# Last stage with sixteen packed expert tiles in place of eighteen, and the first stage's end in another order

## The chip, the cores and the metric

The kernel runs on one core of one Trainium2 chip. The metric is the device time of the whole program in microseconds (us). TensorE is called PE, VectorE DVE, ScalarE ACT, GpSimd POOL and SyncE SP, as in the profile.

## The reference: what is computed

Input is 32 sequences of 750 x 64. Patches of 16 steps with stride 8 become L = 92 tokens of width D = 128 (2944 tokens in all), through a linear layer and a layernorm. Then come two layers, each an attention part and a feed-forward part on a normalized stream, with a residual. Layer 0: a state-space scan with 16 states and a six-expert layer that sends each token to one expert. Layer 1: a local attention with 7 neighbours and 16 heads, and a dense mixture of six experts that this change is about:

```python
probs = softmax(x.mean(axis=1) @ router_w.T)            # one decision per sequence
vals, idx = top_k(probs, 2); vals = vals / vals.sum()
expert_weights = einsum('bk,bke->be', vals, pw[idx])     # 6 weights per sequence
h = gelu(einsum('bsd,edf->ebsf', x, W1) + b1)            # 6 experts, 341 hidden columns each
out_e = einsum('ebsf,efd->ebsd', h, W2) + b2
out = einsum('be,ebsd->bsd', expert_weights, out_e)
```

## The kernel before

Work is tiled in NCH = 8 chunks of 4 sequences (CB = 4, CT = 368 tokens), features on the partitions. Every engine runs its own list in program order, and semaphores tie the lists together. Five stages follow each other, each ended by `stage_end`.

**First stage** (to about 90 us). For each chunk: the patch matmuls (`embed`), a transposition to token-major, a normalization that ACT writes (`embed_norm`), DVE's gamma and beta (`scale_row`, `shift_row`), statistics of the result (`stream_stats`, `stream_moments`), a power on POOL, DVE's `stream_norm`, ACT's `norm_second`, transpositions back, ACT's copies (`norm_copies`), the delta matmul, and on ACT `softplus`. The three chunks in flight are c, c-1, c-2 and c-3 in one turn of the loop. `first_minus` and `first_plus` are ACT exponentials for state 0 of the scan, of which the stage after needs the result; the half for chunks 0 to 3 stands in turn c = 8, behind the softplus of chunk 5. The last things on ACT's list are `softplus(7)`, `first_minus(7, 8)`, and then a table load and the first tanh of the scan stage (L777, L847).

**Last stage** (from about 554 us). In turn c the stage works on attention of chunk c, on the projection, router and first experts of chunk f = c-1, and on the other experts and output of chunks c-2 and c-3.

- PE, in this order: `qkv_of(c)` (L1972), expert tiles of c-2, `project(c-1)` (L1981), more tiles with `result_tm(c-3)` between them (L1953), `scores(c)` (L1991, L1995), tiles, `scores_tm` (L2002), tiles, `shares_fm` (L2008), two tiles, the transpositions of chunk c-1 (L263), then seven steps of `spread_out(c, o)` (L2023, L2024) with tiles between them, `router_spread` (L2033) and tiles.
- An expert of 341 hidden columns is three tiles of 128, 128 and 85. A tile of layer 1 is three matmuls (L1934 to L1936, a number split in high and low parts), a tile of layer 2 is one (L1942, which the trace shows as two records). `FFN` is the list of the 36 tiles of a chunk in the order in which PE takes them, and `ffn(f, lo, hi)` issues a part of it. ACT applies the gelu to each tile of layer 1 (L1008).
- DVE: `weigh_expert` multiplies an expert's output by its weight (L1478), POOL adds it up (L708, `add_expert`). For the attention: the score products (L1509), the softmax (L1524 to L1536, with ACT's exponential and two table loads between them), and for each of seven offsets three products, one of 344 columns and two of 12 for the ends of the sequences (L1599), which POOL adds up (L738). `spread_out(o)` waits until offset o-2 has been read.
- Between the offsets stands the router on tiles of 4 x 11 (L1463, L1457, L1467, L1560 to L1580), and with it `stream_sums`, `weigh_expert` 4 and 5.

Of the kernel before, what the change touches and what calls it, by code (L numbers as in the profile page):

```python
# [7 lines left out]
def audio_tower(nc, t, out):  # L8
# [27 lines left out]
    FT = 3  # L36
    FR = FF - 2 * D
# [24 lines left out]
    with ctx:  # L62
# [203 lines left out]
        def norm_copies(act, nm, u, c, banks, scale=None, bias=None, dst=xfm, hi=None):  # L266
            for w in range(nm.n):
# [48 lines left out]
        split_hi = sb("split_hi", [128, NE * FF], f32r)  # L316
        split_lo = sb("split_lo", [128, NE * FF], f32r)
        w_hi, w_lo = (x[:, 0:8 * D].rearrange("p (s u k d) -> p s u k d", s=2, u=2, k=2) for x in (split_hi, split_lo))
        v1_hi, v1_lo = (x[:, :].rearrange("p (e f) -> p e f", e=NE) for x in (split_hi, split_lo))
# [100 lines left out]
        W_COLS = 3 * D + D + K * 2 * HEADS + K * D + OH + CT + NE * FF + 3 * NE * D + NE + NE + NE * NPART + NE * CB + D  # L420
# [8 lines left out]
        v1 = take(NE, FF)  # L429
        v2 = take(NE, 2, D)  # L430
        v2b = take(NE, D, parts=FR)
        b1b = take(NE, parts=FR)
# [27 lines left out]

        fh = take(3, FT, CT)
        facc = take(CT)
# [13 lines left out]
        ewb = take(NE, CB)  # L476
        bb = take(CB)
# [8 lines left out]
        facc_add = sem("facc_add")  # L486
        f_mm, f_free = sem("f_mm"), sem("f_free")
# [7 lines left out]
               + [(1, e, j) for e in (3, 4) for j in range(FT)] + [(2, e, j) for e in (2, 3) for j in range(FT)]  # L495
               + [(1, 5, 0), (1, 5, 1)] + [(2, 4, j) for j in range(FT)] + [(1, 5, 2)]
               + [(2, 5, j) for j in range(FT)])
# [7 lines left out]
        def _(sp):  # L505
# [42 lines left out]
            for dst, name in ((v1, "v1"), (v2, "v2"), (v2b, "v2b"), (b1b, "b1b"), (b2T, "b2T"), (pwT, "pwT"),  # L548
                              (diag, "diag"), (ones4, "ones4")):
                sp.dma_start(dst, t[name]).then_inc(wF_ready, 16)  # L550
# [54 lines left out]
        def _(pool):  # L605
# [92 lines left out]
            def add_expert(f, e):  # L698
                if not 0 <= f < NCH:
                    return  # L700
                if e == 0 and f:
                    pool.wait_ge(fT_ready, f)
                pool.wait_ge(fo_free, f * NE + e + 3)
                if e:
                    pool.wait_ge(facc_add, f * NE + e + 2)
                a3, t3 = (x.rearrange("p (j l) -> p j l", j=CB) for x in (facc, ftmp[:, e % 2]))
                other = bb.rearrange("p (j o) -> p j o", o=1).to_broadcast([D, CB, L]) if e == 0 else a3
                pool.tensor_tensor(a3, t3, other, ALU.add).then_inc(facc_add, 1)  # L708
# [36 lines left out]
            for c in range(NCH + 2):  # L745
                add_expert(c - 3, 5)
# [4 lines left out]
                add_expert(c - 2, 0)  # L751
# [5 lines left out]
                add_expert(c - 2, 4)  # L757
                if c < NCH:
# [7 lines left out]
        def _(act):  # L766
# [244 lines left out]

# [23 lines left out]
            for c in range(NCH + 2):  # L1035
# [6 lines left out]
                gelus(c - 2, 18, 21)  # L1042
# [3 lines left out]
                gelus(c - 2, 27, 33)  # L1046
# [1150 lines left out]
```

## Time and profile before

| | us |
|---|---|
| median of three runs (857.26 to 857.68) | 857.44 |
| the profiled execution's own time | 858.12 |
| its span | 856.3 |
| PE busy over the span | 632.5 |
| DVE busy | 630.3 |
| ACT busy | 519.7 |
| POOL busy | 268.0 |

Busy time is the union of an engine's instructions; the granted clock of PE is 1.00 at 2.4 GHz and 0.50 at 1.2 GHz. In a row of the order of time the first number is the start and the second the length in us.

### The profile page before, as it was taken

To read this page: it belongs to the slowest core of one execution; us is meant where nothing else is said; L and a number is where in the kernel's file an instruction comes from. 1 tells how busy PE (TensorE), PEld (TensorE's weight loads), DVE (VectorE), ACT (ScalarE), POOL (GpSimd) and SP (SyncE) were. 2 spreads that over 40 slices of the span, in tenths; PEclk is the share of its full clock that TensorE was granted. 3 is DMA by queue.
4 is the path that set the end of the run, shared out by engine and by line. 5 is a ranking of instruction groups with operands and counts; after the bars stand their busy time and mean duration, and the time that the engine had idled before them with its cause. 6 is when DMAs were issued, how large, how long until landed. Compare 5 with 4: busy or idle time off the path is not lost.

```text
span 856.3 us, 10989 instructions
## 1 busy us (share of the span) xinstructions
PE 632.5 (74%) x3150; PEld 484.1 (57%) x3151; DVE 630.3 (74%) x1351; ACT 519.7 (61%) x813; POOL 268.0 (31%) x297
## 2 busy tenths in 40 slices
PE   6994752652816537297773799877999999999987
PEld 4552752652816537274652789534766766766655
DVE  1785597999999999997874112268788888887752
ACT  1587999999899898952322234244465565464432
POOL 0464100000000000101486244314545556464432
PEclk9995776876869677699685799978899999999999
DMA  5380043444455543434112466200000000000000
GB/s 174 113 302 22 0 83 70 77 77 83 83 92 109 93 83 70 75 66 161 68 30 83 115 170 170 60 27 1 1 1 9 1 10 10 1 10 10 0 10 19
DMA packets 26273, 56.51 MB, mean 66 GB/s; under 512 B 4006, under 2 KB 15375, under 8 KB 26004
## 3 DMA queue, kind: packets, MB, share of 16 engines
q0 software_dynamic: 5728, 24.56, 15.2%
q1 hardware_dynamic: 19924, 30.88, 12.0%
q10 hardware_dynamic: 576, 0.52, 0.2%
q8 instruction: 21, 0.34, 0.2%
q14 instruction: 24, 0.20, 0.1%
HBM read 29.89 MB, written 10.17 MB: 47 GB/s over the span
## 4 chain that ended last, share of the span: by engine, by line
PE 42%; DVE 24%; issue 15%; ACT 9%; DMA 3%; POOL 3%; POOLq 1%; SPq 1%; DVEq 0%; ACTq 0%
PE psum L1942 10%; DVE s_R L1197 5%; DVE s_R L1184 4%; PE psum L1672 4%; DVE s_R L1208 3%; PE psum L1934 2%; PE psum L1865 2%; PE psum L1972 2%; DVE s_R L1599 2%; PE psum L1873 2%; DVE s_R L1189 2%; DMA s_R<-x_sorted 2%; PE psum L263 2%; PE psum L1936 2%; PE psum L1995 2%
## 5 line engine op out<-in xcount | busy, mean ns | idle before, releaser
L1736 PE MATMUL psum<-s_xn_lo,s_split_hi 128*128 128x368 f32 x256 | 95.6, 374 | 135.3 <-ACT s_R L882 132.8
L1736 PEld LDWEIGHTS psum<-s_xn_lo,s_split_hi 128*128 128x128 f32 x256 | 55.3, 216 | 140.0 <-ACT s_R L882 135.5
L1942 PE MATMUL psum<-s_R 128*128 128x368 f32 (+1 forms) x288 | 101.2, 477 | 4.1 <-ACT s_R L1008 4.1
L1203 DVE TENSOR_TENSOR_SCAN s_R<-s_R 128x2944 f32<-128x2944 f32 x16 | 100.7, 6291 | 0.8
L650 POOL DMA_DIRECT2D s_xnfm<-s_R x14 | 17.1, 1219 | 255.9 <-DVE s_R L1208 255.9
L1737 PE MATMUL psum<-s_xn_hi,s_split_lo 128*128 128x368 f32 x256 | 92.6, 362 | 0.0
L1738 PE MATMUL psum<-s_xn_hi,s_split_hi 128*128 128x368 f32 x256 | 92.2, 360 | 0.0
L1008 ACT ACTIVATE s_R<-psum,s_cols 128x368 f32<-128x368 f32 x96 | 50.6, 566 | 53.1 <-PE psum L1936 52.8
L708 POOL TENSOR_TENSOR s_R<-s_R 128x368 f32<-128x368 f32 x47 | 44.9, 956 | 74.7 <-DVE s_R L1478 55.0
L1942 PEld LDWEIGHTS psum<-s_R 128*128 128x128 f32 (+1 forms) x288 | 51.2, 189 | 28.6 <-issue 8.2
L738 POOL TENSOR_TENSOR s_R<-s_R 128x368 f32<-128x368 f32 x48 | 46.7, 973 | 57.1 <-DVE s_R L1599 55.7
L889 ACT ACTIVATE s_R<-psum,s_cols 128x736 f32<-128x736 f32 x64 | 55.8, 875 | 13.6 <-PE psum L1738 9.3
L1934 PE MATMUL psum<-s_xn_lo,s_split_hi 128*128 128x368 f32 x144 | 59.2, 411 | 4.8 <-DVE s_xn_lo L1540 2.3
L1184 DVE SCALAR_TENSOR_TENSOR s_R<-s_R 128x2944 f32<-128x2944 f32 x16 | 51.4, 3213 | 9.7 <-ACT s_R L847 5.9
L882 ACT ACTIVATE s_R<-psum,s_cols 128x736 f32<-128x736 f32 x64 | 55.5, 875 | 2.1 <-PE psum L1738 1.4
L1197 DVE SCALAR_TENSOR_TENSOR s_R<-s_R,s_mean 128x2944 f32<-128x2944 f32 x16 | 52.5, 3282 | 5.2 <-ACT s_part L873 3.9
L1737 PEld LDWEIGHTS psum<-s_xn_hi,s_split_lo 128*128 128x128 f32 x256 | 55.2, 216 | 0.0
L1738 PEld LDWEIGHTS psum<-s_xn_hi,s_split_hi 128*128 128x128 f32 x256 | 54.8, 214 | 0.0
L1672 PE MATMUL psum<-s_R 128*128 128x368 f32 x128 | 45.7, 503 | 7.1 <-ACTq L772 7.1
L1208 DVE SCALAR_TENSOR_TENSOR s_R<-s_R,s_A_c 128x2944 f32<-128x2944 f32 x15 | 49.2, 3282 | 0.6
L1936 PE MATMUL psum<-s_xn_hi,s_split_hi 128*128 128x368 f32 x144 | 48.4, 336 | 0.0
L1935 PE MATMUL psum<-s_xn_hi,s_split_lo 128*128 128x368 f32 x144 | 48.4, 336 | 0.0
(245 smaller groups left out, 1562.5 us busy)
## 6 DMA issues: line engine op xcount, KB each, us to landing
s_xnfm<-s_R POOLq DMA_DIRECT2D x14, 1472.0 KB, 10.5
s_R<-in_w SPq DMA_DIRECT2D x28, 256.0 KB, 2.9
s_R<-in_xg SPq DMA_DIRECT2D x7, 744.0 KB, 4.2
x_sorted<-in_x_init SPq DMA_DIRECT2D x1, 5082.0 KB
s_wBC<-in_wBC SPq DMA_DIRECT2D x8, 256.0 KB, 2.7
s_R<-x_sorted SPq DMA_DIRECT2D x28, 66.0 KB
s_R<-in_w SPq DMA_DIRECT2D x1, 1536.0 KB, 6.3
s_R<-y_rows SPq DMA_DIRECT2D x8, 184.0 KB
```

Source lines behind the costliest of these rows:

```text
L889: act.activation(group(bufC, u, h), psum[:, h * HB:(h + 1) * HB, 0:CT], ACT.Silu, bias=cols[:, bass.ds(n + at["C_b"], 1)], scale=1.0).then ...
L1184: dve.scalar_tensor_tensor(th[:, u], ea, 1.0, th[:, u], ALU.add, ALU.mult).then_inc(ea_free, 1)
L1197: dve.scalar_tensor_tensor(bufB[:, u], bufB[:, u], mean[:, u:u + 1], th[:, u], ALU.subtract, ALU.mult).then_inc(th_free, 1)
L1203: dve.tensor_tensor_scan(bufB[:, u], ra[:, u], bufB[:, u], 0.0, ALU.mult, ALU.add).then_inc(ra_free, 1)
L1208: dve.scalar_tensor_tensor(bufC[:, u], bufB[:, u], A_c[:, bass.ds(n, 1)], bufC[:, u], ALU.mult, ALU.mult).then_inc(prod_ready, 1)
L1672: ins = pe.matmul(bank(u).rearrange("p (b l) -> p b l", b=CB), w_emb[:, j, h, :], x4[:, j, :, h:h + L], start=(n == 0), stop=(n == 7))
L1736: pe.matmul(bank(c), w_hi[:, s, u, k, :], xn_lo[:, a:b], start=True, stop=False)
L1737: pe.matmul(bank(c), w_lo[:, s, u, k, :], xn_hi[:, a:b], start=False, stop=False)
L1738: ins = pe.matmul(bank(c), w_hi[:, s, u, k, :], xn_hi[:, a:b], start=False, stop=True)
L1934: pe.matmul(o, w_hi_, fm(xn_lo, f % 2), start=True, stop=False)
L1936: pe.matmul(o, w_hi_, fm(xn_hi, f % 2), start=False, stop=True).then_inc(f_mm, 1)
L1942: ins = pe.matmul(bank((2, 4)[e % 2]), w, fh[0:kk, e % 3, j], start=(j == 0), stop=(j == FT - 1))
```

## The change

Of each expert, the first 256 hidden columns stay as two tiles. The six remainders of 85 columns (510 columns) are packed side by side into NR = 4 tiles of 128, so that a chunk has 12 + 4 = 16 tiles in each layer. A packed tile holds columns of several experts, so its gelu is multiplied by the expert weights before layer 2 (`weigh_rest`, one DVE instruction over 4 x 368 columns, with a mask that gives each hidden column its expert's weights), and the four packed tiles of layer 2 add up to a seventh unit whose output ACT copies out (`rest_out`). The output bias b2 moves into `weigh_expert`. PE's tiles and the others' lists are dealt out anew. PE gets three matmuls without a reader in front of `shares_fm` from turn 2 on, and some in the last turns of the first stage. The two products for the ends of an offset become one. In the first stage ACT's `first_minus(0, NP)` moves in front of `embed_norm(7)`, `first_plus(0, NP)` in front of `norm_second(6)`, and DVE's work on chunk 7 in front of `stream_norm(6)`.

```diff
+        FFN: ... [(1, 3, 0), (1, 3, 1)] + [(1, NE, r) for r in range(NR)]
+               + [(1, 4, 0), (1, 4, 1)] + [(2, e, j) for e in (2, 3) for j in range(FT)]
+               + [(1, 5, 0), (1, 5, 1)] + [(2, e, j) for e in (4, 5) for j in range(FT)]
+               + [(2, NE, r) for r in range(NR)])
 # ACT, first stage
                 if c == NCH - 1:
+                    act.wait_ge(A_ready, 1)
+                    first_minus(0, NP)
                     embed_norm(c)
+                if c == NCH:
+                    first_plus(0, NP)
                 if c >= 2:
                     norm_second(act, nA, c % 2, c - 2)
...
-                if c == NCH:
-                    act.wait_ge(A_ready, 1)
-                    first_minus(0, NP)
-                    first_plus(0, NP)
 # DVE, first stage
+                if c == NCH:
+                    scale_row(c - 1) ... shift_row ... stream_stats ... stream_moments(c - 1)
                 if 0 <= c - 2 < NCH:
                     stream_norm(c - 2)
 # PE, first stage
+                if c >= NCH - 1:
+                    keep_busy_1(1 if c == NCH - 1 else 2)
                 if c >= 3:
                     delta(c - 3)
...
+                if NCH - 1 <= c < NCH + 2:
+                    keep_busy_1(2)
                 if 0 <= c - 2 < NCH:
                     norm_transposes(pe, nA, c % 2, c - 2, (4, 5))
 # DVE, last stage
-                for lo, at_k in ((0, o), (E1, L - K + o)):
-                    yield (o3[:, :, lo:lo + E0], q3[:, :, lo:lo + E0],
-                           k3[:, :, at_k:at_k + 1].to_broadcast([128, CB, E0]))
+                yield both_ends(o3, 0, E1, 1), both_ends(q3, 0, E1, 1), both_ends(k3, o, L - K, 0)
...
+                dve.scalar_tensor_tensor(ftmp..., bank((2, 4)[g % 2])..., b2T[:, e:e + 1], w, ALU.add, ALU.mult)
...
+            def weigh_rest(f):
+                dve.wait_ge(f_free, 2 + tile_no1(f, NE, NR - 1) + 1)
+                dve.tensor_tensor(r3, r3, w, ALU.mult).then_inc(fr_weighed, 1)
...
+                    if not att:
+                        weigh_rest(f - 1)
                 weigh_expert(f - 1, 0)
...
+                weigh_expert(f - 1, 4)
                 if tail:
                     split_stream(f)
                 for o in range(K):
                         if tail:
                             stream_sums(f)
-                        weigh_expert(f - 1, 4)
+                        weigh_expert(f - 1, 5)
+                        if att:
+                            weigh_rest(f - 1)
...
-                    if o == 5 and tail:
+                    if o == 4 and tail:
                         router_weights(f)
 # PE, last stage
-                ffn(f - 1, 18, 20)
+                ffn(f - 1, 14, 16)
+                ffn(f - 1, 16, 18)
                 if tail:
                     project(f)
-                ffn(f - 1, 20, 21)
+                ffn(f - 1, 18, 19)
                 result_tm(c - 3)
-                ffn(f - 1, 21, 22)
+                ffn(f - 1, 19, 20)
                     scores(c)
-                ffn(f - 1, 22, 24)
+                ffn(f - 1, 20, 22)
                     scores_tm(c)
-                ffn(f - 1, 24, 33)
+                ffn(f - 1, 22, 26)
+                    if c >= 2:
+                        fill_pause(3)
                     shares_fm(c)
-                ffn(f - 1, 33, 35)
                     norm_transposes(pe, nF, f % 2, f, (5, 5))
+                ffn(f - 1, 26, 28)
                 for o in range(K):
                         spread_out(c, o)
-                    if o == 0:
-                        ffn(f - 1, 35, NF)
-                    else:
-                        ffn(f, 2 * o - 2, 2 * o)
+                    elif 1 <= o <= 3:
+                        ffn(f, 2 * o - 2, 2 * o)
+                    elif o == 4:
+                        ffn(f - 1, 28, 30)
+                    elif o == 5:
+                        ffn(f - 1, 30, NF)
+                        ffn(f, 6, 8)
+                    elif o == 6:
+                        ffn(f, 8, 10)
+                        if tail:
+                            router_spread(f)
+                        ffn(f, 10, 12)
...
-                ffn(f, 12, 15)
-                if tail:
-                    router_spread(f)
-                ffn(f, 15, 18)
+                ffn(f, 12, 14)
```

## Rows read from the trace of the kernel before

**Rows 1.** The page, busy time by engine over the span.
```profile
PE 632.5 (74%) x3150; PEld 484.1 (57%) x3151; DVE 630.3 (74%) x1351; ACT 519.7 (61%) x813; POOL 268.0 (31%) x297
```
**Rows 2.** Busy in stretches: PE, PEld, DVE, ACT, POOL, granted clock, DMA share, GB/s.
```profile
64.50:91.50 27.00, 15.40 (x47) 10.37 (x48) 13.34 (x52) 21.66 (x44) 11.97 (x12) 0.50 0.03 13
...
679.62:712.57 32.95, 31.63 (x166) 21.91 (x165) 28.24 (x92) 18.44 (x35) 18.94 (x21) 1.00 0.03 7
...
745.52:778.45 32.93, 31.63 (x165) 21.91 (x165) 28.05 (x92) 18.42 (x35) 18.86 (x21) 1.00 0.02 6
```
**Rows 3.** PE in order of time, turns 1, 5 and 8; brackets hold idle time before.
```profile
613.34 2.02 PE L1972 MATMUL psum<-s_xfm,s_R 128*128 128x368 f32 x6
...
718.53 1.44 PE L1995 MATMUL psum<-s_R 128*32 128x368 f32 x14
...
727.78 1.48 PE L1942 MATMUL psum<-s_R 128*128 128x368 f32 x4 [0.43 <-ACT s_R L1008]
...
729.37 0.41 PE L2023 MATMUL psum<-s_xn_lo,s_xn_hi 112*128 112x368 f32 x1
...
730.13 0.61 PE L2023 MATMUL psum<-s_xn_lo,s_xn_hi 112*128 112x368 f32 x1
...
735.34 0.37 PE L2023 MATMUL psum<-s_xn_lo,s_xn_hi 112*128 112x368 f32 x1
...
745.36 2.02 PE L1972 MATMUL psum<-s_xfm,s_R 128*128 128x368 f32 x6
...
822.09 1.48 PE L1942 MATMUL psum<-s_R 128*128 128x368 f32 x4 [0.75 <-ACT s_R L1008]
```
**Rows 4.** Groups of the last stage: busy us, mean ns, idle before.
```profile
L1942 PE MATMUL psum<-s_R 128*128 128x368 f32 x192 | 70.9, 480 | 4.1 <-ACT s_R L1008 4.1
L1934 PE MATMUL psum<-s_xn_lo,s_split_hi 128*128 128x368 f32 x96 | 39.4, 411 | 2.8 <-DVE s_xn_lo L1540 2.3 <-ACT s_R L1008 0.2
L1599 DVE TENSOR_TENSOR s_R<-psum,s_R 128x344 f32<-128x344 f32 x56 | 28.6, 511 | 5.6 <-PE psum L2024 3.8 <-POOL s_R L738 1.3
L1478 DVE TENSOR_TENSOR s_R<-psum,s_R 128x368 f32<-128x368 f32 x48 | 25.6, 538 | 14.3 <-PE psum L1942 13.6
L1599 DVE TENSOR_TENSOR s_R<-psum,s_R 128x12 f32<-128x12 f32 x112 | 13.1, 157 | 0.0
```
**Rows 5.** A long DVE instruction of the scan stage, from the page's groups.
```profile
L1184 DVE SCALAR_TENSOR_TENSOR s_R<-s_R 128x2944 f32<-128x2944 f32 x16 | 51.4, 3213 | 9.7 <-ACT s_R L847 5.9
```
**Rows 6.** DVE in order of time, turn 5.
```profile
715.39 3.07 DVE L1509 TENSOR_TENSOR s_R<-s_R 128x344 f32<-128x344 f32 x7
...
726.61 1.10 DVE L238 TENSOR_SCALAR s_xs<-s_H,s_mv,s_rs 92x128 f32<-92x128 f32 x4
...
730.49 0.54 DVE L1540 TENSOR_TENSOR s_xn_lo<-s_xnfm,s_xn_hi 128x368 fp32r<-128x368 f32 x1 [1.92 <-ACT s_xnfm L273]
...
736.43 1.33 DVE L1467 SCALAR_TENSOR_TENSOR s_R<-s_R,s_prio 4x11 f32<-4x11 f32 x1
...
743.60 1.02 DVE L1587 TENSOR_TENSOR s_R<-s_R 128x24 f32<-128x24 f32 x1
```
**Rows 7.** POOL in order of time, the same turn.
```profile
715.27 3.24 POOL L713 TENSOR_SCALAR s_pa<-s_mv 92x4 f32<-92x4 f32 x1 [2.34 <-DVE s_mv L207]
...
736.76 0.98 POOL L738 TENSOR_TENSOR s_R<-s_R 128x368 f32<-128x368 f32 x1
...
743.60 0.98 POOL L708 TENSOR_TENSOR s_R<-s_R 128x368 f32<-128x368 f32 x1
```
**Rows 8.** ACT in order of time, end of the first stage.
```profile
68.32 1.49 ACT L792 ACTIVATE s_R<-psum,s_R 92x128 f32<-92x128 f32 x4 [2.17 <-POOL s_R L622]
...
82.27 1.28 ACT L250 ACTIVATE s_R<-s_xs,s_rs 92x128 f32<-92x128 f32 x4 [1.07 <-DVE s_xs L238]
...
89.76 1.28 ACT L777 ACT_TABLE_LOAD   x1
```
**Rows 9.** DVE in order of time, end of the first stage.
```profile
75.35 0.68 DVE L1097 TENSOR_TENSOR s_R<-s_R,s_rows 92x512 f32<-92x512 f32 x1
```

More of the change, by code:

```diff
@@ L428, in audio_tower @@
         posc = take(CT, parts=K)
[L429 to L432, printed above, removed]
+        v1 = take(NT1, D)
+        v2 = take(NT1, D)
+        b1r = take(NR)
+        rmask = take(NR, NE)
         b2T = take(NE)
@@ L461, in audio_tower @@
         fh = take(3, FT, CT)
+        fr = take(NR, CT)
+        wr = take(NR, CB)
+        wrt = take(NR, CB, NE)
         facc = take(CT)
@@ L494, in audio_tower, with tile_no1, added, unit_out @@
                + [(2, e, j) for e in (0, 1) for j in range(FT)]
-               + [(1, e, j) for e in (3, 4) for j in range(FT)] + [(2, e, j) for e in (2, 3) for j in range(FT)]
-               + [(1, 5, 0), (1, 5, 1)] + [(2, 4, j) for j in range(FT)] + [(1, 5, 2)]
-               + [(2, 5, j) for j in range(FT)])
+               + [(1, 3, 0), (1, 3, 1)] + [(1, NE, r) for r in range(NR)]
+               + [(1, 4, 0), (1, 4, 1)] + [(2, e, j) for e in (2, 3) for j in range(FT)]
+               + [(1, 5, 0), (1, 5, 1)] + [(2, e, j) for e in (4, 5) for j in range(FT)]
+               + [(2, NE, r) for r in range(NR)])
+        ORDER1 = [(e, j) for layer, e, j in FFN if layer == 1]
+        def tile_no1(f, e, j):
+            return f * NT1 + ORDER1.index((e, j))
+        def added(g):
+            return g // NU * NE + max(g % NU, 1)
+        def unit_out(eng, f, e):
+            if e == NE:
+                eng.wait_ge(fr_out, f + 1)
+            else:
+                eng.wait_ge(fo_free, f * NE + e + 1)
         NF = len(FFN)
@@ L700, in add_expert @@
                     return
[L701 to L708, printed above, removed]
+                g = f * NU + e
+                if e == 1:
+                    unit_out(pool, f, 0)
+                    if f:
+                        pool.wait_ge(fT_ready, f)
+                unit_out(pool, f, e)
+                if e > 1:
+                    pool.wait_ge(facc_add, added(g - 1))
+                pool.tensor_tensor(facc, ftmp[:, g % 2], ftmp[:, 1 - g % 2] if e == 1 else facc, ALU.add)\
+                    .then_inc(facc_add, 1)
             def rstd_e(c):
@@ L1439, in per_head, with both_ends @@
                 return x.rearrange("p j (h o) -> p j h o", o=1).to_broadcast([L, CB, HEADS, K])
+            def both_ends(x3, first, apart, step_l):
+                x = x3[:, :, first:first + E0]
+                return bass.AP(x.tensor, x.offset, list(x.ap[:-1]) + [[apart, 2], [step_l, E0]])
             def windowed(u, o, other, k, op_out):
@@ L1692, in to_fm, with keep_busy_1 @@
                     norm_transposes(pe, nm, u, i * 2 + u, banks)
+            def keep_busy_1(n):
+                for _ in range(n):
+                    pe.matmul(bank(1), wprep[:, 1, :], fm(xnfm, 0), start=True, stop=True)
             pe.sem_inc(delta_read, 2)
@@ L2003, in scores_tm, with fill_pause @@
                 ins.then_inc(ST_ready, 1)
+            def fill_pause(n):
+                for _ in range(n):
+                    pe.matmul(bank(3), w_proj, w_qkv.rearrange("p k d -> p (k d)")[:, 0:CT], start=True, stop=True)
             def shares_fm(c):
@@ L2074, in _ @@
                     norm_transposes(pe, nE, c % 2, c + 1, (7, 7))
-                ffn(f, 12, 15)
-                if tail:
+                ffn(f, 12, 14)
+                if tail and not att:
                     router_spread(f)
-                ffn(f, 15, 18)
             result_last()
```

166 lines of the change are left out of this document (107 added, 59 removed).

## The prediction

> **What bounds the kernel now.** I read the busy times by engine first [rows 1]: PE and DVE are level at 74%, so no engine bounds the whole, and each stage must be read by itself. The stretches of the last stage come next [rows 2]: a turn in steady state takes 32.95 us, PE is busy for 31.63 of it at a granted clock of 1.00 (2.4 GHz), DVE for 28.24. PE in order of time [rows 3] shows that it hardly waits: the idle times in a turn add up to about 1.5 us (the largest are 0.43 in front of the layer-2 tiles at 727.78 and some 0.5 in front of one spread). So PE's list sets the turn, with DVE 4 us behind it. I cut a turn at three marks. S is the end of the score matmuls (718.53 + 1.44 = 719.97). T is the first spread, at 729.37 = S + 9.40. Q is the next `qkv_of`, at 745.36 = S + 25.39. The next S is at S + 32.95, so Q to S is 7.56. In the first stage it is ACT's list that ends last (its table load for the scan stands at 89.76), after waits of 2.17 and 1.07 us [rows 8], while PE runs at 0.50 (1.2 GHz) from 64.5 to 91.5 [rows 2].
>
> **Fewer tiles.** A layer-2 matmul is two records, and they follow each other every 0.31 us; at 727.78 four of them take 1.48 with the tail of the last (0.62 a tile, issue to issue). The three matmuls of a layer-1 tile take 0.50. A chunk loses two tiles of each layer: 2 x 0.62 + 2 x 0.50 = 2.24 us of PE. If PE stayed the only limit, that would be 18 us over eight chunks. But the tiles are also dealt out anew, and that has to be followed through the turn.
>
> **S to T.** After the scores PE now has two layer-2 tiles (1.24), the transposition of scores (0.42), two layer-1 tiles (1.3 with 0.27 for the switch between the two kinds) and two layer-2 tiles (1.24): S + 4.2. Then come the three fillers, 1.86: S + 6.1. `shares_fm` needs the softmax, whose last DVE instruction begins 0.85 before 726.61 and is out at S + 6.73 [rows 6]. Nothing of the change shortens that: it goes scores, ACT copy, table load, exponential, three DVE instructions. So the fillers are free (hidden in a pause of 2.6), but the real work that stood there is gone from it. The transpositions of chunk c-1 now stand in front of two tiles and wait for `normed_f`, whose end is 726.61 + 1.10 = S + 7.74. With 0.3 and 1.3 for these, T is S + 9.4, as before: a pause has taken the place of the work that was taken out.
>
> **T to Q.** Here DVE now leads up to offset 2, since `spread_out(4)` waits for it. `split_stream` can start at S + 9.27 (ACT's copies after the transpositions), 1.25 earlier than the S + 10.52 of 730.49 [rows 6]. Offset 0 can be read 0.67 after T. Then: offset 0 0.52, sums 0.45, `weigh_expert(5)` 0.5, `weigh_rest`, offset 1 0.52, `router_largest`, offset 2 0.52. The price of `weigh_rest` isn't in the trace. From below it is 4 x 0.44 - 3 x 0.08, the score products of 344 columns at 3.07/7 each [rows 6] less three starts, 1.5; from above 1472/2944 x 3.21 = 1.61 plus a start [rows 5], 1.7. I take 1.6. Merging the ends saves one instruction of two; the small one steps by 0.07 in the trace and lasts 157 ns [rows 4], so 0.05 an offset, 0.4 a turn (bounds 0 and 1.1). The bias in `weigh_expert` costs 0 to 0.1 each beside 0.54 [rows 4]; I take 0.05.
>
> DVE and POOL block each other on tiles in SBUF. The L1587 of 24 columns took 1.02 beside a POOL add of 0.98 that began with it, the 4 x 11 instruction at 736.43 took 1.33 and ended with POOL's add of 736.76, and POOL's small L713 took 3.24 behind DVE's seven products [rows 6, 7]. In the new order `weigh_expert(4)` stands in front of `split_stream`, so POOL's add of it starts 0.1 to 0.2 before the split and holds it until S + 10.05: 0.4 late. And `weigh_rest` holds POOL's next add until it is done, so that this add and the one of offset 1 stand against `router_largest` (1.05 alone, 1.55 as before, 2.0 at worst). Offset 2 ends at S + 15.3 with no blocking, S + 16.65 with all of it. I take S + 16.0.
> The Trainium skill (SBUF — State Buffer, Who interferes with whom) says that a DVE instruction with two inputs in SBUF contends with a POOL instruction that reads SBUF, and that the loser fully blocks. The trace agrees (1.02 for an instruction of 24 columns). By that rule both places block, and the turn would be 0.65 longer than I take.
>
> PE meanwhile issues three spreads and six layer-1 tiles and waits for offset 1 and then offset 2, 0.7 and 0.5 to 1. From spread 4 on it is alone: that spread 0.44, two packed tiles 1.24, spread 5 0.62 (a spread behind layer-2 tiles costs 0.61 to its second matmul's turn, [rows 3]), four tiles 2.48, spread 6 0.62, two tiles 1.24, `router_spread` 0.33, two layer-1 tiles 1.12, the transpositions 0.33, two packed layer-1 tiles 1.1: 9.5. Q is S + 16.0 + 0.1 + 9.5 = S + 25.6, against S + 25.39.
>
> **Q to S.** 7.56 before; one layer-1 tile more (0.50), one layer-2 tile more (0.62), and four layer-1 tiles in a row behind `qkv_of`, which wait for the gelus behind ACT's three copies, about 0.3: 9.0.
> A turn is thus 25.6 + 9.0 = 34.6; since the softer values are all on the slow side I take 34.4, 1.45 more than now. Bounds: 33.9 (no blocking) less 0.3, and 35.2.
>
> **Both ends of the last stage.** In turn 1 there are no tiles of an older chunk, so the new order only has less: Q comes at about 610.9 where it was 613.34 [rows 3], -2.5; Q to S gives back 1.25. Then five turns from S to S, +7.25, and a T to Q, +0.2. In turns 8 and 9 PE has 2.24 less, and the waits for the third gelu (0.75 at 822.09 and again in turn 9, [rows 3]) go; but `weigh_rest` stands in front of `weigh_expert(0)` there and the second-layer tiles wait for it, 0.45 and 1.3, and the transpositions of chunk 7 wait for the residual, some 1.5. Net -0.6 (bounds -3 and +1). Sum: -2.5 + 1.25 + 7.25 + 0.2 - 0.6 = +5.6. The two gelus fewer on ACT and the added copy, the loads (the same bytes within 0.1 MB) and the expert weights over 96 columns instead of 24 (+0.1) stand beside the path.
>
> **First stage.** `first_minus(0, 4)`, 1.41, moves into the wait of 2.17 [rows 8], since softplus(3) is done before it. DVE's work on chunk 7 began at 75.35 [rows 9] behind a delta at half clock; now it begins when `embed_norm(7)` is done, at 69.8. `stream_norm(7)` ends at about 77.3 (82.25 before). From there ACT has no waits but 0.7 and some 0.3: of the 5 us in which it idled between 66.1 and 89.76, 3.4 go. The load comes at 86.3, and the scan stage follows it. The fillers stand in front of waits; at half clock two take 2.5 instead of 1.24 and could push the delta of chunk 5 by 0.6. Bounds -2 and -4.
>
> **Sum.** From the profiled execution, 858.12 - 3.4 + 5.6 = 860.3; it lies 0.68 above the median, so on the median's scale 857.44 + 2.2 = 859.6. I say 859.6.
>
> **Rivals.**
> (a) The spreads don't wait for DVE. If split, router and `weigh_rest` slip between POOL's adds and PE gets its offsets in time, a turn is PE's own list, 31.45 - 2.24 = 29.2, plus the pause in front of the shares, 2.6, and 0.6 for `normed_f`: 32.4, 0.55 less than now. Then the last stage gives -2.5 + 1.25 - 2.75 - 0.5 - 0.6 = -5.1, and with the first stage 849.0. For it: PE has always been the engine in front here. Against it: 1.6 us more on DVE exactly between offsets 0 and 1. It would need offset 2 to end by S + 13.8, 1.5 before my best case for it; it decides if my chain from S to offset 2 is too long by that.
> (b) No blocking: turn 33.9, last stage +2.8, 856.8.
> (c) The granted clock falls. PE has 1.4 us of pause around the shares even with the fillers, then 1.2 among the offsets. If it drops to 0.50 for a stretch in some turns, each costs some 1 us: 864. Against it: the turns now hold 1.5 us of idle time and stay at 1.00 [rows 2].
> The Trainium skill (TensorE: Matmul & The Clock Gate, What's actually happening) says that activity releases the throttle and its lack brings it back. In this trace PE ran at 0.50 through 27 us in which it was busy for 15.4 [rows 2], and at 1.00 through the turns; by the rule the fillers keep the sum above and leaving them out would not.
> (d) The first stage gains nothing, since the fillers at half clock stand in front of the transpositions: 863.0.
>
> **Chances.** Forecast 0.42, (a) 0.22, (b) 0.18, (c) 0.09, (d) 0.09. A difference under 0.2% (1.7 us) is what a measurement can't tell from none. (a) is faster; (b) straddles the lower bound, 0.08 faster and 0.10 same; the forecast has 0.29 slower and 0.13 same; (c) and (d) are slower. Faster 0.30, same 0.23, slower 0.47. The likeliest case's own range is 857.5 to 862; for 8 in 10 the range takes in most of (a) and (c): 849.5 to 864.
>
> **What would show it.** A turn of 34.4 with S to T 9.4 unchanged; PE idle in front of spreads 3 and 4, released by DVE L1599's successor; `split_stream` lengthened beside a POOL add; ACT's table load near 86.3. A turn under 33 or PE without waits among the offsets would make it wrong.

## The result, and the profile after

| | us |
|---|---|
| kernel before, median of 5 runs beside it (855.78 to 857.68) | 857.26 |
| changed kernel, median of 5 runs (860.53 to 862.6) | 861.18 |
| ratio, with its 95% interval | 1.0048 (1.0032 to 1.0065) |
| own time and span of the profiled execution | 860.53, 858.7 |

The changed kernel is slower by 0.48%, 3.9 us (2.7 to 5.6 by the interval of the ratio), where 859.6 was predicted, +2.2. These are the same stretches and a steady turn in the changed kernel (columns as in [rows 2]).

```profile
64.50:91.50 27.00, 19.05 (x81) 12.56 (x80) 14.11 (x51) 24.78 (x45) 11.92 (x12) 0.92 0.04 15
606.17:640.17 34.00, 31.12 (x157) 21.43 (x157) 29.22 (x84) 17.40 (x35) 20.21 (x21) 1.00 0.00 1
...
709.02:743.46 34.44, 31.57 (x161) 21.81 (x161) 30.28 (x86) 17.43 (x35) 20.63 (x21) 1.00 0.02 6
```

A turn, from one `qkv_of` (now L2047) to the next, takes 34.44 us where it took 32.95 [rows 3], with two tiles fewer in each layer. DVE is busy for 2 us more. PE in order of time in turn 5 says where the time is (S, the end of the scores at 716.71 + 1.44, is 718.15):

```profile
716.71 1.44 PE L2070 MATMUL psum<-s_R 128*32 128x368 f32 x14
...
722.08 2.02 PE L2082 MATMUL psum<-s_R 128*128 128x368 f32 x6
724.80 0.53 PE L2087 MATMUL psum<-s_ident,s_R 92*112 92x92 f32 x4 [0.70 <-DVE s_R L1591]
725.83 0.54 PE L265 MATMUL psum<-s_ident,s_xs 92*128 92x92 f32 x4 [0.49 <-DVE s_xs L240]
...
727.19 0.61 PE L2102 MATMUL psum<-s_xn_lo,s_xn_hi 112*128 112x368 f32 x1
...
732.02 0.44 PE L2102 MATMUL psum<-s_xn_lo,s_xn_hi 112*128 112x368 f32 x1 [0.64 <-DVE s_R L1655]
...
734.38 0.43 PE L2102 MATMUL psum<-s_xn_lo,s_xn_hi 112*128 112x368 f32 x1 [0.74 <-DVE s_R L1655]
```

L2082 is the fillers. Then PE waits for the shares (0.70), the norm (0.49), offset 1 (0.64, spread 3) and offset 2 (0.74, spread 4). Idle time in a turn was 32.95 - 31.63 = 1.32; now it is 34.44 - 31.57 = 2.87, of which the four waits are 2.57.

Where the other matmuls' time went can be added up from the trace: for each kind of matmul, the time from its start to the start of the next matmul, less the idle time.

| in turn 5, us | before | changed |
|---|---|---|
| idle | 1.32 | 2.87 |
| layer 1 | 10.66 | 9.43 |
| layer 2 | 10.99 | 9.39 |
| fillers | 0 | 2.02 |
| spreads | 3.15 | 3.68 |
| all others | 6.82 | 7.04 |
| turn (the rows are rounded) | 32.95 | 34.44 |

The layers give 2.83. The fillers take 2.02 of it, the spreads 0.53 (three of them now stand right behind layer-2 tiles, and such a one has 0.61 in its row), the others 0.22, and the idle time is 1.55 longer: +1.49. DVE and POOL between the first spread and offset 2:

```profile
727.27 1.11 DVE L1595 TENSOR_TENSOR s_xn_lo<-s_xnfm,s_xn_hi 128x368 fp32r<-128x368 f32 x1 [0.34 <-ACT s_xnfm L275]
...
729.77 1.68 DVE L1535 TENSOR_TENSOR s_R<-s_R 128x1472 f32<-128x1472 f32 x1
731.37 0.59 DVE L1655 TENSOR_TENSOR s_R<-psum,s_R 128x344 f32<-128x344 f32 x2
...
732.32 0.92 DVE L1512 SCALAR_TENSOR_TENSOR s_R<-s_R,s_prio 4x11 f32<-4x11 f32 x1
```
```profile
727.01 0.98 POOL L727 TENSOR_TENSOR s_R<-s_R 128x368 f32<-128x368 f32 x1 [3.95 <-DVE s_R L1525]
729.93 2.35 POOL L727 TENSOR_TENSOR s_R<-s_R 128x368 f32<-128x368 f32 x1 [1.94 <-DVE s_R L1525]
732.24 0.97 POOL L758 TENSOR_TENSOR s_R<-s_R 128x368 f32<-128x368 f32 x1
```

`weigh_rest` (L1535) takes 1.68, holds POOL's add for 2.35, and POOL's next add (732.24) holds the router's 4 x 11 instruction for 0.92.

In the first stage ACT's table load moved from 89.76 to 85.88, and the wait of 2.17 in front of L812 [rows 8] is 0.56; 0.5 of the 3.9 was already there at 52 us, ahead of anything that was edited (in edges_only below, whose first stage is the old one, the load stands at 88.98, so two executions of the same stage differ by 0.8).

```profile
67.78 1.50 ACT L812 ACTIVATE s_R<-psum,s_R 92x128 f32<-92x128 f32 x4 [0.56 <-POOL s_R L640]
...
85.88 1.28 ACT L797 ACT_TABLE_LOAD   x1
```

### The profile page after: what moved, and what is told of

The parts are those of the page before. It is cut to its first block, busy times and chain, and to the rows that moved or that the text cites. A ratio compares the mean times of both kernels' runs of the same rounds, so it can differ in the third digit from the quotient of the medians.

```text
span 858.7 us, 10915 instructions
## 1 busy us (share of the span) xinstructions
PE 628.2 (73%) x3132; PEld 481.7 (56%) x3133; DVE 644.8 (75%) x1303; ACT 512.0 (60%) x805; POOL 281.3 (33%) x297
## 4 chain that ended last, share of the span: by engine, by line
PE 42%; DVE 22%; issue 14%; ACT 14%; POOL 3%; DMA 2%; POOLq 1%; SPq 0%; DVEq 0%; ACTq 0%; another core or an unknown queue 0%
PE psum L2014 7%; PE psum L1732 3%; DVE s_R L1229 3%; DVE s_R L1242 3%; PE psum L1933 3%; PE psum L1941 3%; PE psum L1804 2%; PE psum L2047 2%; PE psum L1805 2%; DVE s_R L1253 2%; PE psum L1806 2%; PE psum L2001 2%; DVE s_xs L240 2%; PE psum L265 2%; PE psum L2070 2%
## 5 line engine op out<-in xcount | busy, mean ns | idle before, releaser
L1804 PE MATMUL psum<-s_xn_lo,s_split_hi 128*128 128x368 f32 x256 | 94.3, 368 | 137.4 <-ACT s_R L902 134.7
L2014 PE MATMUL psum<-s_R 128*128 128x368 f32 x256 | 91.0, 482 | 2.5 <-DVE s_R L1525 2.5
L1805 PE MATMUL psum<-s_xn_hi,s_split_lo 128*128 128x368 f32 x256 | 91.6, 358 | 0.0
L1806 PE MATMUL psum<-s_xn_hi,s_split_hi 128*128 128x368 f32 x256 | 91.3, 356 | 0.0
L727 POOL TENSOR_TENSOR s_R<-s_R 128x368 f32<-128x368 f32 x47 | 53.9, 1147 | 71.6 <-DVE s_R L1525 50.1
L758 POOL TENSOR_TENSOR s_R<-s_R 128x368 f32<-128x368 f32 x48 | 47.8, 997 | 54.9 <-DVE s_R L1655 53.4
L2014 PEld LDWEIGHTS psum<-s_R 128*128 128x128 f32 x256 | 46.3, 192 | 24.6 <-issue 4.7
L2001 PE MATMUL psum<-s_xn_lo,s_split_hi 128*128 128x368 f32 x128 | 50.1, 391 | 3.3 <-ACT s_R L1035 2.1
L1732 PE MATMUL psum<-s_R 128*128 128x368 f32 x128 | 45.0, 497 | 7.2 <-ACTq L792 7.2
L1452 DVE CAST s_R<-s_R 128x1 f32 (+1 forms) x28 | 4.3, 154 | 54.0 <-PE psum L1912 54.0
L867 ACT ACTIVATE s_R<-s_R,s_A_half 128x2944 f32<-128x2944 f32 x16 | 43.8, 2740 | 0.0
```

What stands on the lines that cost most here:

```text
L1732: ins = pe.matmul(bank(u).rearrange("p (b l) -> p b l", b=CB), w_emb[:, j, h, :], x4[:, j, :, h:h + L], start=(n == 0), stop=(n == 7))
L1804: pe.matmul(bank(c), w_hi[:, s, u, k, :], xn_lo[:, a:b], start=True, stop=False)
L1805: pe.matmul(bank(c), w_lo[:, s, u, k, :], xn_hi[:, a:b], start=False, stop=False)
L1806: ins = pe.matmul(bank(c), w_hi[:, s, u, k, :], xn_hi[:, a:b], start=False, stop=True)
L2001: pe.matmul(o, v1_hi[:, n], fm(xn_lo, f % 2), start=True, stop=False)
L2014: ins = pe.matmul(bank((2, 4)[g % 2]), v2[:, n], fr[:, j] if e == NE else fh[:, e % 3, j], start=(j == 0), stop=(j == tiles - 1))
```

## The experiments

Each ran five rounds against the kernel before. A ratio is to that kernel's runs beside it, whose medians were 856.0 to 857.3, so ratios and the steady turn are compared, not the us of different rows. The steady turn is read from the one profiled execution, from one `qkv_of` to the next.

| kernel | median | ratio (95%) | steady turn |
|---|---|---|---|
| before | | 1 | 32.95 |
| changed | 861.18 | 1.0048 (1.0032 to 1.0065) | 34.44 |
| first_only | 853.97 | 0.9972 (0.9952 to 0.9993) | 32.95 |
| edges_only | 852.22 | 0.9951 (0.9934 to 0.9968) | 32.31 |
| old_tiles | 852.09 | 0.9943 (0.9924 to 0.9961) | 32.29 |
| rest_quarter | 852.49 | 0.9944 (0.9924 to 0.9964) | 33.29 |
| rest_early | 850.42 | 0.9930 (0.9904 to 0.9955) | 32.83 |
| no_fill_pause | 868.33 | 1.0138 (1.0104 to 1.0171) | 35.79 |
| pause_tiles | 841.85 | 0.9836 (0.9818 to 0.9855) | 31.82 |
| w4_behind | 862.03 | 1.0059 (1.0042 to 1.0075) | 34.38 |
| no_kb1 | 861.53 | 1.0054 (1.0035 to 1.0074) | 34.45 |
| tail_rest | 857.02 | 0.9996 (0.9982 to 1.0010) | 34.44 |
| pause_and_tail | 842.69 | 0.9828 (0.9810 to 0.9845) | 31.82 |
| ends_apart | 862.53 | 1.0064 (1.0043 to 1.0084) | 34.55 |

**first_only.** Of the whole change, the kernel before gets only the edits of the first stage.

> The kernel before with the new order of the first stage alone (first_minus in turn 7, DVE's chunk 7 ahead of stream_norm, the seven fillers keep_busy_1); the last stage is the old one. Theory: the two parts of the change are independent, the first stage gives 3.3 to 3.4 us, ACT's table load stands at 86.4, and the whole is 857.3 - 3.4 = 853.9. Rival: what the first stage gains is lost again in the stages behind it or was drift between executions: 856.5 to 857.5.

```profile
86.45 1.28 ACT L777 ACT_TABLE_LOAD   x1
```

ACT's load is 3.31 earlier, or 2.5 against the 88.98 of edges_only. The ratio says -2.4 us (-4.1 to -0.6), so the gain reaches the end; its size lies between 2.5 and 3.3 as far as the traces tell.

**rest_quarter.** It leaves out the weighing of three of the four packed tiles, so its output is not the reference's.

```diff
-                r3 = fr.rearrange("p r (j l) -> p (r j) l", j=CB)
+                r3 = fr[:, 0:1].rearrange("p r (j l) -> p (r j) l", j=CB)
-                w = wr.rearrange(...).to_broadcast([D, NR * CB, L])
+                w = wr[:, 0:1].rearrange(...).to_broadcast([D, CB, L])
```

> The changed kernel, but weigh_rest multiplies one of the four packed tiles instead of all four (three tiles go unweighed into layer 2), so it lasts about 0.45 instead of 1.68 us at the same place. Theory: DVE's chain from the score products to offset 2 is what PE waits for ahead of spreads 3 and 4 (0.64 + 0.74 in a turn). With 1.24 us less in it, and POOL's add beside it free sooner, nearly all of these waits go: a turn of 34.28 - 1.3 = 33.0, six turns -7.8, the two waits for weigh_rest in the last two turns -1.2: 861.2 - 9.0 = 852.2. Rival 1: the turn is PE's own list in its new order, DVE's chain is incidental: 860 to 861. Rival 2: half of the waits come from the blocking between POOL and the router's small instructions, which stays: turn -0.7, 856.

PE's waits in a steady turn of this kernel, for the shares, the norm and offset 2:

```profile
721.54 0.53 PE L2087 MATMUL psum<-s_ident,s_R 92*112 92x92 f32 x4 [0.70 <-DVE s_R L1591]
722.56 0.54 PE L265 MATMUL psum<-s_ident,s_xs 92*128 92x92 f32 x4 [0.50 <-DVE s_xs L240]
729.97 0.43 PE L2102 MATMUL psum<-s_xn_lo,s_xn_hi 112*128 112x368 f32 x1 [0.36 <-DVE s_R L1655]
```

`weigh_rest` now takes 0.53. The wait before spread 3 has gone, half of that before spread 4 stays, and the turn is 1.15 shorter. DVE's chain to offset 2 is what PE waits for: rival 1 falls. Of rival 2 the blocking stays, since POOL's add still holds the router's L1512 for 0.93, but its price doesn't: the turn lost 1.15, not 0.7.

**rest_early.**

```diff
                 weigh_expert(f - 1, 2)
+                if att:
+                    weigh_rest(f - 1)
...
                         weigh_expert(f - 1, 5)
-                        if att:
-                            weigh_rest(f - 1)
```

> The changed kernel with weigh_rest (in turns with attention) moved from behind weigh_expert(5), between offsets 0 and 1, to behind weigh_expert(2), ahead of the softmax, where DVE waits 1.14 us for the transposed scores. Nothing else differs. Theory: 1.68 leaves the chain from the softmax to offset 2 and 0.5 comes into it ahead of the softmax, so shares_fm and the first spread are 0.5 later (S + 9.5), offset 2 ends at S + 14.8, and PE's own list (first spread to spread 4 in 5.8 without waits) becomes the limit: spread 4 at about S + 15.4 instead of 16.2; a turn -0.9, six turns -5.4: 855.8. Rival: DVE is simply full (30.2 us busy in 34.3), so it doesn't matter where the 1.68 stands: 860.5 to 861.5.

```profile
719.56 0.53 PE L2086 MATMUL psum<-s_ident,s_R 92*112 92x92 f32 x4 [0.86 <-DVE s_R L1591]
720.57 0.54 PE L265 MATMUL psum<-s_ident,s_xs 92*128 92x92 f32 x4 [0.48 <-DVE s_xs L240]
...
727.47 0.33 PE L2101 MATMUL psum<-s_xn_lo,s_xn_hi 112*128 112x368 f32 x1
```

Both waits among the spreads have gone, and the turn is 1.6 shorter (0.9 expected), with the whole 1.68 still done and DVE as busy (30.76 of 32.83). So a full DVE isn't the cause; the place of `weigh_rest` is. (The third line is spread 4, with no wait before it.) I had priced the delay of the softmax at 0.5; the wait in front of the shares shows 0.16 (0.86 against 0.70). The router's L1512 takes 0.22 here where it took 0.92, but the L1502 two instructions on takes 0.72 where it took 0.22, so from offset 1 to offset 2 DVE needs 2.14 us instead of 2.35: most of the block has only moved. This version of the changed kernel, with one call moved, is faster than the kernel before.

**no_fill_pause.**

```diff
-                    if c >= 2:
-                        fill_pause(3)
```

> The changed kernel without the three filler matmuls in front of shares_fm. Theory: they end 0.7 us before the shares are ready, so without them nothing comes earlier and the time stays at 861.2 (860.5 to 862), if the granted clock stays at 1.00 over a pause of 2.6 us. Rival 1: the clock falls in the turns, some 1 us each: 867. Rival 2: the fillers hold PE or the PSUM bank against real work: 858 to 860.

```profile
731.18 0.53 PE L2087 MATMUL psum<-s_ident,s_R 92*112 92x92 f32 x4 [2.55 <-DVE s_R L1591]
```
```profile
729.00:731.00 2.00, 0.00 (x0) 0.00 (x0) 1.93 (x3) 1.99 (x4) 0.44 (x1) 1.00 0.00 0
731.00:733.00 2.00, 1.33 (x9) 1.15 (x10) 1.89 (x7) 0.55 (x2) 0.00 (x0) 0.82 0.00 0
733.00:735.00 2.00, 2.00 (x6) 1.17 (x5) 1.11 (x2) 0.84 (x2) 0.96 (x1) 0.50 0.00 0
```

The pause is 2.55, about 0.70 + 1.86: the fillers took nothing. Without them the granted clock falls to 0.50 (1.2 GHz) behind the idle stretch, and the turn takes 35.79, 1.35 more (35.6 to 36.0 in the others). Rival 1 holds, and rival 2 falls.

**pause_tiles.**

```diff
+               + [(1, 5, 0), (1, 5, 1)] + [(2, 4, j) for j in range(FT)]
+               + [(2, NE, r) for r in range(NR)] + [(2, 5, j) for j in range(FT)])
...
-                ffn(f - 1, 22, 26)
+                ffn(f - 1, 22, 30)
                 if att:
-                    if c >= 2:
-                        fill_pause(3)
                     shares_fm(c)
...
                     elif 1 <= o <= 3:
+                        if o == 1:
+                            ffn(f - 1, 30, NF)
                         ffn(f, 2 * o - 2, 2 * o)
                     elif o == 4:
-                        ffn(f - 1, 28, 30)
+                        ffn(f, 6, 8)
```

> rest_early, and the four packed layer-2 tiles moved from behind spreads 4 and 5 into the pause ahead of shares_fm, in place of the three fillers; expert 5's two layer-2 tiles move from ahead of the first spread to behind spread 1, the unit order becomes 0,1,2,3,4,packed,5, ACT's rest_out follows the gelus of expert 5, POOL's last add stands in its own turn. Theory: in rest_early PE's list sets the turn (32.87, of it 1.86 of fillers and 1.34 of idle time around shares_fm), and the saved tiles only come back if real work stands in that pause. Behind spread 4, which waits for offset 2 (S + 15), 2.48 go; DVE's list (30.8 busy in 32.83, some waits unavoidable) becomes the limit: a turn of 31.4, six turns -9: 841.5. Rival: DVE's chain catches up at once, since offset 6 and the router close the turn: 32.5, 848.

```profile
700.14:731.96 31.82, 29.51 (x156) 20.57 (x156) 30.17 (x86) 17.63 (x35) 19.98 (x21) 1.00 0.02 7
```
```profile
714.39 2.75 PE L2012 MATMUL psum<-s_R 128*128 128x368 f32 x8 [1.04 <-DVE s_R L1524]
717.07 0.53 PE L2085 MATMUL psum<-s_ident,s_R 92*112 92x92 f32 x4
718.09 0.54 PE L265 MATMUL psum<-s_ident,s_xs 92*128 92x92 f32 x4 [0.49 <-DVE s_xs L240]
...
730.02 0.40 PE L2110 MATMUL psum<-s_R 4*128 4x24 f32 x2 [0.39 <-DVE s_R L1634]
```

The four packed tiles (714.39) now fill the pause, PE has 29.51 busy and DVE 30.17 of 31.82, and the whole is 1.6% faster than before. The turn is 0.4 longer than expected, and the time comes out all the same: the end of the stage is shorter than in rest_early (last `qkv_of` to the last group of matmuls 69.9 against 74.4). Between the two profiled executions (848.5 and 838.5) turns 2 to 6 give 5.8 us and that end 4.5. The edit changes the order of the tiles in both, and no run takes it apart further.

**edges_only.** The kernel before with the two ends in one instruction, in `windowed`.

> The kernel before, with the two ends of each offset (and of the score products) in one instruction instead of two, nothing else. Theory: DVE is 0.05 an offset shorter, 0.35 a turn, and PE, whose list sets the turn, gains at most the part of its waits that hang on an offset: a turn 32.8 to 32.95, in all 0 to -1 us against before, so no difference that can be measured. Rival: the strided instruction is slower than two short ones: +0.5 a turn, +3.

The wait in question in a turn of before, who waited for the offsets' instruction (us, times; L1599 of before and L1601 here), and a turn of this kernel:

```profile
738.96 0.44 PE L2023 MATMUL psum<-s_xn_lo,s_xn_hi 112*128 112x368 f32 x1 [0.50 <-DVE s_R L1599]
```

```profile
L1599 DVE TENSOR_TENSOR s_R<-psum,s_R x168: 148/160/520, 572.6 to 808.3; 128x12 f32<-128x12 f32 x112, 128x344 f32<-128x344 f32 x56
...
  PE psum L2023: 2.9, 6
```
```profile
L1601 DVE TENSOR_TENSOR s_R<-psum,s_R x112: 160/336/519, 571.1 to 802.1; 128x344 f32<-128x344 f32 x56, 128x24 f32<-128x24 f32 x56
...
  PE psum L2025: 0.8, 3
```
```profile
708.06:740.37 32.31, 31.48 (x166) 21.98 (x166) 27.72 (x86) 18.44 (x35) 18.93 (x21) 1.00 0.03 7
```

My expectation was wrong: the turn is 0.63 shorter and the whole 4.2 us (2.7 to 5.7), not nothing. The wait of 0.5 in front of one spread, which the prediction itself mentions, hung on an offset, and it is gone: PE's idle time in the turn is 0.83 instead of 1.32, and its waits for offsets in the whole stage fell from 2.9 to 0.8 us. (In one of the five steady turns, 32.77 us long, a wait of 0.29 for an offset stays.) I had called PE the only limit because its idle time was small, and the merged ends took half a microsecond of just that.

**w4_behind.**

```diff
-                weigh_expert(f - 1, 4)
                 if tail:
                     split_stream(f)
+                weigh_expert(f - 1, 4)
```

> The changed kernel with weigh_expert(4) behind split_stream instead of ahead of it, so that POOL's add of expert 4 no longer starts with split_stream. Theory: split_stream lasts 0.67 instead of 1.11, offsets 1 and 2 and with them spreads 3 and 4 come 0.44 earlier, a turn 34.0: -2.6 over six turns, 858.5. Rival: the add then starts beside offset 0 or stream_sums and holds those back by as much: no change, 861.

```profile
731.49 0.54 DVE L1595 TENSOR_TENSOR s_xn_lo<-s_xnfm,s_xn_hi 128x368 fp32r<-128x368 f32 x1 [0.86 <-ACT s_xnfm L275]
731.95 0.59 DVE L1525 SCALAR_TENSOR_TENSOR s_R<-psum,s_R 128x368 f32<-128x368 f32 x1
```

`split_stream` drops from 1.11 to 0.54, so the blocking is real. But DVE now waits 0.86 for ACT instead of 0.34: `weigh_expert(4)` had filled 0.52 of that wait, and now it comes behind it. 0.57 gained and 0.52 lost leave 0.05, and the turn changes by 0.06. The rival had the result right and the reason wrong: the add now stands beside `stream_sums` and `weigh_expert(5)`, and these take 0.53 and 0.59 (0.52 and 0.59 in the changed kernel).

**no_kb1.** The changed kernel without the seven fillers of the first stage.

> The changed kernel without the seven filler matmuls of the first stage. Theory: the first stage's gain comes from the order on DVE and ACT; the fillers only raise the clock behind 73 us, which shortens the last transpositions, the delta and the state matmuls: without them ACT's table load is 0.5 to 1 later (86.5 to 87) and the time +0.7: 861.9. Rival 1: the fillers stand in front of waits for nothing: load 0.3 earlier. Rival 2: the gain is the fillers' (the clock): load at 89.

The load stands at 85.85 (85.88 with them), and the intervals of the ratios overlap: they change nothing that can be measured, and the gain of that stage is the order on ACT and DVE. No run takes the edits on these two engines apart.

**tail_rest.**

```diff
                     expert_weights(f - 1)
-                    if not att:
-                        weigh_rest(f - 1)
...
                 if tail:
                     normed_f(f)
+                if not att:
+                    weigh_rest(f - 1)
```

> The changed kernel with weigh_rest of the two turns without attention moved from ahead of weigh_expert(0) to behind normed_f; the six turns with attention are untouched. Theory: there the second-layer tiles stand behind a multiplication of 1.69 us that itself waits for four gelus (waits of 0.67 and 1.53 ahead of the tiles), and the transpositions of chunk 7 then wait 1.82 for the residual's norm. Without it: -0.7 - 0.9 in turn 8, -1.5 in turn 9, in all -2.5 to -3: 861.2 - 2.8 = 858.4. This is the term that the prediction had at -0.6 and that came out near +1.5. Rival: another wait of the same size takes its place (the router's decision, the gelus): -0.5, 860.7.

The changed kernel's waits in the last two turns:

```profile
816.89 0.89 PE L2014 MATMUL psum<-s_R 128*128 128x368 f32 x2 [0.67 <-DVE s_R L1525]
...
824.72 0.88 PE L265 MATMUL psum<-s_ident,s_xs 92*128 92x92 f32 x4 [1.82 <-DVE s_xs L240]
...
843.97 0.89 PE L2014 MATMUL psum<-s_R 128*128 128x368 f32 x2 [1.53 <-DVE s_R L1525]
```

and what is left of them in tail_rest:

```profile
825.46 0.54 PE L265 MATMUL psum<-s_ident,s_xs 92*128 92x92 f32 x4 [1.18 <-DVE s_xs L240]
827.57 2.75 PE L2014 MATMUL psum<-s_R 128*128 128x368 f32 x8 [0.30 <-DVE s_R L1525]
```

From the last `qkv_of` (777.92 and 780.21) to the start of the last matmuls (853.84 and 851.84) it is 75.92 and 71.63 us: 4.3 less, more than expected, with the turns as they were. The waits shown add up to 4.02 and 1.48, so they give 2.5. Another 1.2 is the granted clock. Behind the wait of 1.82 it falls to about half, and behind the 1.18 of tail_rest it stays at 1.00 (changed kernel, then tail_rest):

```profile
824.72:828.00 3.28, 3.28 (x9) 2.21 (x10) 1.45 (x3) 0.85 (x2) 0.96 (x1) 0.53 0.02 5
```
```profile
825.46:828.74 3.28, 2.98 (x12) 1.79 (x13) 3.28 (x5) 0.85 (x2) 3.14 (x2) 1.00 0.02 5
```

The same transpositions and twelve layer-2 records take 5.34 us there and 4.11 here (idle time taken off). The fall stands at the same place, behind 1.81 to 1.82 us of waiting, in rest_early, w4_behind, no_kb1 and ends_apart too (granted clock 0.50 to 0.67 in the 3.28 us behind it).

**pause_and_tail.**

> pause_tiles and tail_rest together (in the turns without attention the packed layer-2 tiles stand behind the transpositions of chunk c-1 again). Theory: 841.9 - 2.5 = 839.4, if the two are independent. Rival: in pause_tiles the tail is bound elsewhere: 841.5.

The ratios of the two kernels with packed tiles in the pause overlap. In this one the four packed tiles of turn 8 wait 1.16 us for `weigh_rest`, right behind a wait of 1.17 for the norm, and the granted clock behind them is 0.54; from the last `qkv_of` to the last group of matmuls it takes 71.1 us, against 69.9 in pause_tiles. The rival holds: the edit that gave 4.3 on the changed kernel gives nothing there, and in the trace it costs 1.2.

**ends_apart.** The changed kernel with `windowed` as it was before.

> The changed kernel with the two ends of each offset and of the score products in two instructions again. Theory: DVE's chain from the softmax to offset 2 holds three offsets, each 0.06 longer, and PE waits for it: a turn 34.44 + 0.2 = 34.6, up to 35.1 if the score products (0.5 a turn for seven) shift the softmax too: +1.2 to +4, likeliest 863.5. Rival: the merged ends give in the changed kernel what they gave alone in the kernel before (0.63 a turn, 4.2 in all): 865.4.

A turn is 34.55, 0.11 longer; the medians can't tell the two. The same edit is worth 0.63 a turn in the old order and 0.11 in the new one, so the rival falls. (The two turns of this trace that took 35.77 and 36.24 are left out; they are in the last section.)

**old_tiles.** first_only and edges_only together, with the eighteen tiles a layer.

> The kernel before (eighteen tiles a layer, old placement) with the first stage's new order and the merged ends: the whole change without the packing of the experts. Theory: -3.3 and -4.2 add up: 857.3 - 7.5 = 849.8, so the packing with its placement costs 11 us, and packing with weigh_rest moved (rest_early, 850.4) is worth nothing against it; only with real tiles in the pause (pause_tiles) is it worth 8. Rival: the two gains overlap (both were partly the state of the clock): 852.

-4.9 us (-6.5 to -3.3) by the ratio; 7.2 by the spans of the two profiled executions (849.1 against 856.3). The medians fit the rival better, the steps in the trace (load at 86.24, turn 32.29) the theory; whether the two gains add up in full stays open. Either way all that the change lost lies in the packing and its placement: 1.0048 against 0.9943, some 9 us. And rest_early can't be told from old_tiles (0.9930 against 0.9943): of the kernels run here, packing pays only in the two with real tiles in the pause.

## Why the prediction was right where it was, and where it was not

The prediction was right in its mechanism: PE waits for DVE's chain to offset 2, and `weigh_rest` makes that chain too long. Here is the sum by its own steps, in the two profiled executions (marks: `qkv_of` of the turns, and the start of the last matmuls on PE):

| stretch | predicted | measured |
|---|---|---|
| up to the first `qkv_of` | -3.4 | -3.9 |
| turn 0 | 0 | -0.5 |
| turn 1 | -2.5 | -2.7 |
| turns 2 to 6 | +7.25 | +6.8 |
| turn 7 to the end | +0.85 | +3.0 |
| sum | +2.2 | +2.7 |

- **First stage**: right in cause, and in size as far as it can be told (-2.5 to -3.3 by ACT's load in first_only). The fillers that I feared and credited did neither harm nor good. The agreement up to the first `qkv_of` (-3.4 and -3.9) proves less than it seems: in the twelve kernels with the new order of this stage that `qkv_of` starts anywhere from 551.5 to 555.0, and in the two with the old one at 555.6 and 554.5. That scatter arises in the stages between, and its cause stays open.
- **S to T**: 9.4 predicted unchanged, 9.04 measured. The fillers lie in the pause as said, 0.70 of it left.
- **T to Q**: the waits stand before spreads 3 and 4, 0.64 and 0.74 where I had 0.7 and 0.5 to 1; offset 2 ends at S + 16.2 (16.0). `weigh_rest` 1.68 (1.6). rest_quarter and rest_early show that this chain is the cause.
- **Blocking**: the place behind `weigh_rest` is real (L1512 0.92 here, 0.22 in rest_early), but only 0.2 of that is gone from the chain in rest_early, since the block moves to an instruction behind it. The one at `split_stream` is real too (1.11 against 0.54), but costs the turn 0.06 at most, since taking it away opens a wait for ACT. I counted 0.4 for it; what I had wrong was mainly that it lies on the path.
- **Q to S**: 9.1 (9.0).
- **Turn**: 34.44 (34.4).
- **The tail** is the term that failed: -0.6 predicted, within bounds of -3 and +1. With turn 7 up to its end at +1.45, as I had it, +3.0 leaves +1.55, outside them. I had both waits for `weigh_rest` (0.45 and 1.3; 0.67 and 1.53 measured) and the wait for the norm (1.5; 1.82); together they came out 0.8 larger. What I had put at nothing is the granted clock, which falls behind the longest of these waits and costs 1.2. 0.8 and 1.2 are about the 2.15 by which the term was off. tail_rest takes 2.5 us of the waits and the fall away by moving that one instruction, and gives 4.3.
- **Merged ends**: 0.05 an offset is about the right size (ends_apart: 0.11 in a turn whose chain holds three), but I let it count only in the new chain. In the old order it is worth 0.63 a turn.
- **Rivals**: (a) fell because offset 2 ends 2.4 later than it needed. (b) fell by its number: the turn is 34.44, not 33.9. But the blocking is only part of what makes it so: of the 0.5 between them the two places give about 0.06 and 0.2. (c) didn't happen in turns 2 to 7 of this trace, but it did in turn 8, where it cost 1.2, and in single turns of two other kernels (below). (d) fell.

That the sum in the profiled executions comes within 0.5 us (+2.2 and +2.7) is partly luck: the tail was 2.15 too low, and the other four stretches together were 1.65 too high. The misses of three of these (all but turns 2 to 6) are no larger than what executions of the same code differ by. Turn 1 is an example: the old last stage took 33.90 in before and 32.55 in first_only. The changed kernel's took 31.17, while six of the kernels derived from it had 30.3 to 30.4 with the same code in that turn or nearly so. On the scale of the medians the forecast of +2.2 lies just below the interval of 2.7 to 5.6: right in direction, and about half the size.

## What to carry to other kernels

Work taken off the busiest engine was a gain here only where real work moved into the pauses that it left. The saved tiles became fillers and waits until the packed tiles were put in front of the softmax's result, and one call moved into a wait of DVE made the difference between 0.5% slower and 0.7% faster. Before pricing a new instruction, list what stands behind it up to the next place where another engine waits, and look for an idle gap of its engine with the inputs ready: here its place mattered more than its length. A wait of PE can cost more than its length: behind the waits of 1.82 us in turn 8 and of 2.55 us in no_fill_pause the granted clock fell each time. Small waits of an engine that is busy for 96% of a turn aren't noise; they say who sets the last half microsecond.

## What the runs showed of the hardware

**A product with one input from PSUM isn't held by POOL's adds; one with two inputs from SBUF is.** In the changed kernel an offset beside a POOL add keeps its 0.60 (two instructions), where the split with both inputs in SBUF takes 1.11 instead of 0.54.

```profile
734.50 0.61 DVE L1655 TENSOR_TENSOR s_R<-psum,s_R 128x344 f32<-128x344 f32 x2
```
```profile
734.40 0.98 POOL L758 TENSOR_TENSOR s_R<-s_R 128x368 f32<-128x368 f32 x1 [1.19 <-DVE s_R L1655]
```

The Trainium skill (SBUF — State Buffer, Who interferes with whom) says that a DVE instruction with at most one SBUF input, outside certain modes, doesn't contend with GpSimd, and one with two does when GpSimd reads SBUF. The trace agrees in both. Being small doesn't help either: the router's 4 x 11 instruction L1512 takes 0.92 beside an add here and 0.22 in rest_early. And one input from SBUF isn't always safe: the router's TENSOR_SCALAR on a 4 x 11 tile takes 1.23 beside another POOL add of the same turn, and 0.22 where no add runs.

```profile
735.62 1.23 DVE L1502 TENSOR_SCALAR s_R<-s_R 4x11 f32<-4x11 f32 x1
```

What a row can't tell is whether the block lies on the path; w4_behind had to.

**The granted clock falls now and then in turns that usually keep it.** Of the steady turns of w4_behind one took 36.01:

```profile
642.84:678.85 36.01, 33.00 (x161) 22.83 (x161) 30.57 (x86) 17.41 (x35) 21.48 (x21) 0.95 0.02 6
678.85:713.22 34.37, 31.38 (x161) 21.86 (x161) 28.86 (x86) 17.41 (x35) 19.55 (x20) 1.00 0.02 7
```

The same instructions and the same idle time of PE (3.0), but 1.6 us more at a mean granted clock of 0.95; ends_apart has two such turns (35.77 and 36.24, against 34.55). In all three the fall stands right behind the waits before spreads 3 and 4, which in this turn of w4_behind end at 665.77 (0.88) and 668.12 (0.74):

```profile
668.00:670.00 2.00, 1.88 (x4) 1.40 (x5) 1.90 (x8) 0.01 (x1) 1.85 (x3) 0.55 0.02 4
```

So the waits that `weigh_rest` makes cost more than their length in some turns, and why in these and not in the others stays open. Turn 1 varies by 1.4 between executions of the same code, and the stages before the last one scatter by up to 3.5 us, so one profiled execution can be off by several us. Outside such falls the steady turns of one trace agree within 0.1 us (edges_only and old_tiles have one turn each that is 0.5 longer), and are steadier than medians.
